# A cross network on one core: x0 transposed from the gathered rows, its rows repeated by DMA, first layer-1 chunk two banks later

## The chip, the core and the metric

One core of a Trainium2 chip. Its engines run their own queues and meet at semaphores: TensorE (PE, with its weight loads PEld), VectorE (DVE), ScalarE (ACT), GpSimd (POOL) and SyncE (SP), which here only issues DMAs. The metric is the time of one launch in microseconds on the device, median of several runs. A single execution was also recorded by the hardware profiler, and all rows below come from it.

## What is computed

A batch of 1024 samples. For each, 39 embedding rows of 16 numbers are gathered from 39 tables (x0: 39 x 16). Three layers of a compressed interaction network follow, then a small dense tower:

```python
for W in [f0, f1, f2]:                       # W: (39*g, 128), g = 39, 128, 128
    z = einsum('bfd,bgd->bfgd', x0, xk).reshape(b, 39 * g, d)
    xk = einsum('bpd,pm->bmd', z, W)         # 128 maps of 16 numbers
    outs.append(xk)
z = sum(concatenate(outs, axis=1), axis=-1)  # (b, 384)
h = relu(concatenate([z, dense_ctx]) @ W_top1 + b_top1)
h = relu(h @ W_top2 + b_top2)
y = h @ W_top3
```

## The kernel before

The kernel works on columns (sample, d). A batch is 128 samples, 2048 columns; there are 8. A batch has 4 groups of 512 columns, and a group has 4 tiles of 128 columns. `step(bt, u, last)` is one tile on each engine: TensorE, VectorE and ScalarE run u = 0 and 1 of batch 0, then a loop of seven batches with u = 2 to 17, then the rest. Within a step ten banks q = 0 to 9 follow each other, and the tables of pairs at the top of the file, (tile in the group, bank) or (u, bank), say behind which bank an extra piece of work is put. So the order is written out by hand, engine by engine.

Layer 2, `cin2`, is the bulk: for a tile, y = x1 times the weights of four fields, in three matmuls of 512 columns per bank (high and low parts, L456, L457, L460; the tenth bank has 384). Banks live in a ring of five (`RING`), so bank n waits until bank n-5 has been used up. Banks 0, 3, 5 and 7 are scaled by ScalarE (`scale`, L664), the others by VectorE in multiply-adds (`mac`, L809), four per bank. GpSimd adds up the 16 terms (`add_up`, L351, L355) into x2; `terms` and x2 have two buffers, so the sum of tile u must be there before ScalarE scales tile u+2. VectorE's second bank waits for ScalarE's first.

Layer 1, `cin1`, is for the next group: seven chunks k of 117 rows, each the product of two factors of x0. `x0_cols` holds x0 by columns with its 39 fields repeated cyclically, 123 rows, so that factor k is rows k to k+117. SP moves the factors: `move_first` (three DMAs, into `x0_first`, which ScalarE copies to PSUM, L643) and `move` (six DMAs into `prods`, L292). VectorE multiplies (`multiply`, L781) at the places `PRODUCTS`, ScalarE splits three of them (L648), GpSimd makes the low parts (L219), and TensorE does the chunks at the places `CIN1`: the first at (1, 6), which waits for all seven products (L424). Three chunks take three short matmuls, the others one fp32 matmul.

Layer 3 goes through `sum_s3` (L470) and, once per batch, `cin3` (L480).

The x0 of the next batch: GpSimd gathers one table after the other into `x0_in` (L328), 39 gathers spread over the sums of 15 tiles, u = 10 to 24. At (9, 3) ScalarE copies the rows three times and a bit into `x0_rows` (`put_aside`, L605 and L607; L704 and L838 in the prologue), which frees `x0_in`. At the four places `TURNS`, TensorE transposes them, four transposes each (`turn`, L404, out 123 rows), and ScalarE stores the columns (`store_cols`, L616; `store_first_cols`, L623, in the prologue). SP's queue in the loop: for each group `move`, with `move_first` of the next, then `move_diag`, eight DMAs; ahead of group 4 it loads the ids of the batch after next.

## Time and profile before

| | us |
|---|---|
| median of 3 runs | 1400.6 (1400.31 to 1401.37) |
| the profiled execution | 1401.89 |
| its span | 1400.1 |
| TensorE busy | 1297.8 |
| GpSimd busy | 1040.9 |
| VectorE busy | 981.8 |
| ScalarE busy | 773.4 |

Some 52 us at the start are the serial gathers of batch 0 and some 60 at the end are the dense tower; between them the program is periodic, with eight batches of four groups. The granted clock of TensorE is 1.00 of its full speed nearly throughout. A busy TensorE is not one at its peak: matmuls overlap, and a row's duration is longer than its distance to the next.

### The profile page before, as it was taken

To read this page: it belongs to the slowest core of one execution; us is meant where nothing else is said; L and a number is where in the kernel's file an instruction comes from. 1 tells how busy PE (TensorE), PEld (TensorE's weight loads), DVE (VectorE), ACT (ScalarE), POOL (GpSimd) and SP (SyncE) were. 2 spreads that over 40 slices of the span, in tenths; PEclk is the share of its full clock that TensorE was granted. 3 is DMA by queue.
4 is the path that set the end of the run, shared out by engine and by line. 5 is a ranking of instruction groups with operands and counts; after the bars stand their busy time and mean duration, and the time that the engine had idled before them with its cause. 6 is when DMAs were issued, how large, how long until landed. Compare 5 with 4: busy or idle time off the path is not lost.

```text
span 1400.1 us, 25243 instructions
## 1 busy us (share of the span) xinstructions
PE 1297.8 (93%) x5629; PEld 982.7 (70%) x5629; DVE 981.8 (70%) x3243; ACT 773.4 (55%) x2449; POOL 1040.9 (74%) x921
## 2 busy tenths in 40 slices
PE   0199999999999999999999999999999999999999
PEld 0167677876787777777777777777778777777754
DVE  2078778586877878587876878688786878688720
ACT  2146666356646665467655566466664576456631
POOL 7668888686887878788886888788786866566530
PEclk9999999999999999999999999999999999999999
DMA  8122121110211121011211112111211101111000
GB/s 218 36 82 55 47 59 53 37 43 24 59 54 51 46 59 53 5 53 46 60 53 51 46 33 58 28 53 46 60 52 52 46 12 55 45 51 45 1 1 0
DMA packets 72379, 67.51 MB, mean 48 GB/s; under 512 B 32140, under 2 KB 44402, under 8 KB 72260
## 3 DMA queue, kind: packets, MB, share of 16 engines
q1 hardware_dynamic: 59556, 62.38, 15.0%
q0 software_dynamic: 9984, 2.58, 1.9%
q10 hardware_dynamic: 2720, 1.48, 0.4%
q14 instruction: 107, 0.88, 0.2%
q8 instruction: 12, 0.20, 0.1%
HBM read 10.15 MB, written 0.00 MB: 7 GB/s over the span
## 4 chain that ended last, share of the span: by engine, by line
PE 65%; DVE 15%; issue 10%; POOL 5%; ACT 2%; DMA 1%; DVEq 1%; SPq 0%; ACTq 0%; POOLq 0%
PE ps L456 13%; PE ps L460 13%; PE ps L457 13%; PE ps L435 13%; DVE terms L809 10%; PE ps L480 5%; DVE prods L781 4%; POOL x_in L328 3%; PE ps L470 3%; PE ps L545 2%; ACT terms L664 2%; PE ps L404 2%; POOL terms L351 2%; PE ps L555 1%; DVEq L808 1%
## 5 line engine op out<-in xcount | busy, mean ns | idle before, releaser
L809 DVE SCALAR_TENSOR_TENSOR terms<-ps,x_scal,terms 128x128 f32<-128x128 f32 x2944 | 814.8, 344 | 294.2 <-PE ps L460 182.6
L664 ACT ACTIVATE terms<-ps,x_scal 128x128 f32<-128x128 f32 x2048 | 586.1, 375 | 388.9 <-PE ps L460 359.8
L351 POOL TENSOR_TENSOR terms<-terms 128x1024 f32<-128x1024 f32 (+2 forms) x384 | 565.6, 1473 | 173.7 <-DVE terms L809 152.9
L456 PE MATMUL ps<-w_high,x_high 128*128 128x512 f32 (+1 forms) x1280 | 581.6, 454 | 3.8 <-ACT terms L664 1.7
L460 PE MATMUL ps<-w_high,x_low 128*128 128x512 f32 (+1 forms) x1280 | 498.7, 390 | 1.1 <-ACT x_rows L607 1.1
L457 PE MATMUL ps<-w_low,x_high 128*128 128x512 f32 (+1 forms) x1280 | 498.3, 389 | 0.0
L328 POOL DMA_INDIRECT x_in<-in_tbl,ids_now x312 | 299.8, 961 | 97.7 <-issue 86.1
L456 PEld LDWEIGHTS ps<-w_high,x_high 128*128 128x128 f32 x1280 | 240.9, 188 | 97.1 <-DVE terms L809 21.7
L457 PEld LDWEIGHTS ps<-w_low,x_high 128*128 128x128 f32 x1280 | 241.6, 189 | 73.5 <-issue 29.8
L460 PEld LDWEIGHTS ps<-w_high,x_low 128*128 128x128 f32 x1280 | 240.9, 188 | 54.5 <-ACT x_rows L607 2.0
L435 PE MATMUL ps<-prods,w 117*128 117x512 f32 x262 | 135.3, 602 | 5.0 <-DVE prods L781 5.0
L781 DVE TENSOR_TENSOR prods<-prods,ps 117x512 f32<-117x512 f32 x192 | 130.4, 679 | 2.3 <-DMA prods<-x_cols 2.3
L219 POOL TENSOR_TENSOR prods_low<-prods,prods_high 117x512 fp32r<-117x512 f32 x93 | 119.0, 1296 | 16.4 <-DMA ids_now<-in_ids 8.6
L470 PE MATMUL ps<-x_diag,x 128*128 128x320 f32 x256 | 89.5, 431 | 0.0
L648 ACT ACTIVATE prods_high<-prods 117x512 fp32r<-117x512 f32 x93 | 60.5, 651 | 42.7 <-DVE prods L781 42.7
L480 PEld LDWEIGHTS ps<-s,w 128*128 128x128 f32 x624 | 73.1, 192 | 2.4 <-issue 0.5
L480 PE MATMUL ps<-s,w 128*128 128x128 f32 x624 | 73.2, 275 | 0.0
L355 POOL TENSOR_TENSOR x<-terms 128x128 f32<-128x128 f32 x128 | 58.9, 460 | 17.8 <-POOL terms L351 14.5
L435 PE MATMUL ps<-prods_high,w_high 117*128 117x512 f32 x93 | 39.8, 428 | 33.2 <-DVE prods L781 30.5
L404 PE MATMUL ps<-eye,x_rows 128*123 128x128 f32 x128 | 29.1, 360 | 39.3 <-ACT x_rows L704 39.3
L435 PEld LDWEIGHTS ps<-prods,w 117*128 117x128 f32 x262 | 50.0, 193 | 22.1 <-issue 7.6
L404 PEld LDWEIGHTS ps<-eye,x_rows 128*123 128x123 f32 x128 | 30.0, 299 | 41.0 <-issue 39.8
(49 smaller groups left out, 525.7 us busy)
## 6 DMA issues: line engine op xcount, KB each, us to landing
prods<-x_cols SPq DMA_DIRECT2D x192, 234.0 KB
x_first<-x_cols SPq DMA_DIRECT2D x96, 78.0 KB
x_in<-in_tbl,ids_now POOLq DMA_INDIRECT x312
x_diag<-x_scal SPq DMA_DIRECT2D x256, 9.8 KB
s<-in_f SPq DMA_DIRECT2D x3, 832.0 KB, 13.3
wt<-in_W_top ACTq DMA_DIRECT2D x1, 768.0 KB, 8.1
wt<-in_W_top ACTq DMA_DIRECT2D x1, 512.0 KB, 9.3
terms<-in_w_pair SPq DMA_DIRECT2D x1, 409.5 KB
```

The source lines that it names most:

```text
L219: eng.tensor_tensor(prods_low[:, i, :], prods[0:KR, SPLIT[i], :], prods_high[:, i, :].bitcast(F32), ALU.subtract).then_inc(low_ready(gf, i ...
L328: pool.indirect_dma_start(out=x0_in[:, f, :], out_offset=None, in_=tables[f], in_offset=bass.IndirectOffsetOnAxis(ap=ids_now[:, f:f + 1], ...
L351: nc.gpsimd.tensor_tensor(t[:, 0:n], t[:, 0:n], t[:, n:2 * n], ALU.add).then_inc(s_tree, 1)
L435: mm = nc.tensor.matmul(ps[:, X1_BANK, :], w, x, start=(k == order[0] and n == 0), stop=(k == order[-1] and n == len(passes) - 1))
L456: nc.tensor.matmul(y, x1_high[:, par, at:at + P], high, start=True, stop=False)
L457: nc.tensor.matmul(y, x1_high[:, par, at:at + P], low, start=False, stop=False)
L460: nc.tensor.matmul(y, x1_low[:, par, at:at + P], high, start=False, stop=True) \
L470: nc.tensor.matmul(ps[:, S3_BANK, 0:TB * FX], x2[:, u % 2, :], x0_diag[:, j % 2, t].rearrange("p b f -> p (b f)"), start=True, stop=True). ...
L480: mm = nc.tensor.matmul(ps[:, MISC_BANK, 0:BATCH], w2[:, f, :], s3[:, f, :], start=(f == 0), stop=(f == F - 1))
L664: op = nc.scalar.activation(terms[:, u % 2, FB * ACT_BANKS.index(q) + i, :], ps[:, (BANKS * u + q) % RING, i * G:(i + 1) * G], ACT.Copy, s ...
L781: nc.vector.tensor_tensor(prods[0:KR, k, :], second, ps[0:KR, bank, :], ALU.mult) \
L809: nc.vector.scalar_tensor_tensor(out=acc, in0=y, scalar=x0, in1=acc, op0=ALU.mult, op1=ALU.add).then_inc(s_mac, 1)
```

## The change

Three edits. The transposes read `x0_in` directly, 39 columns each, and `x0_rows`, `put_aside` and VectorE's copies go. `x0_cols` gets rows 0 to 38 from the store, and SP copies them to rows 39 to 77, 78 to 116 and 117 to 122 by three DMAs (`repeat`) and waits for them; in the prologue first for the 512 columns of group 0, then for the other 1536. Since `x0_in` is now in use until the fourth turn, GpSimd's gathers wait for that (`s_turn`) and are spread over u = 11 to 24. Five of the seven places of `CIN1` move: the first from (1, 6) to (1, 8).

```diff
-CIN1 = ((1, 6), (1, 9), (2, 2), (2, 5), (2, 8), (3, 1), (3, 4))
+CIN1 = ((1, 8), (2, 1), (2, 4), (2, 6), (2, 8), (3, 1), (3, 4))
...
-ROWS_AT = (9, 3)
+GATHERED, SUMMED = 8, 10
...
+            def repeat(cols, n):
+
+                for i in range(1, SPT + 1):
+                    rows = min(F, CYCLIC - i * F)
+                    sp.dma_start(x0_cols[i * F:i * F + rows, cols], x0_cols[0:rows, cols]).then_inc(s_cyc, 16)
+                sp.wait_ge(s_cyc, n * (16 * SPT))
...
                 if j == 0:
                     sp.wait_ge(s_cols, 4)
+                    repeat(slice(GCOLS, BATCH * D), 2)
                 if j % GROUPS < GROUPS - 1:
                     move_first(j + 1)
...
             sp.wait_ge(s_cols, 1)
+            repeat(slice(0, GCOLS), 1)
             move(0, 0)
...
                 load_ids(bt + 2)
+                sp.wait_ge(s_cols, bt * 4 + 8)
+                repeat(slice(0, BATCH * D), bt + 3)
                 move(bt * GROUPS + GROUPS, GROUPS)
...
             pool.wait_ge(s_ids, 2 * 16)
-            pool.wait_ge(s_rows, 3)
-            wanted, ahead = ROWS_AT[0], 12
+            pool.wait_ge(s_turn, 4)
+            ahead = 12
...
             with pool.Fori(0, NBATCH - 2) as bt:
                 pool.wait_ge(s_ids, (bt + 3) * 16)
-                pool.wait_ge(s_rows, bt * 2 + 5)
-                add_up(bt, wanted)
-                for n in range(STEPS - 1):
-                    for f in share(0, n, STEPS - 1):
-                        gather(f)
-                    add_up(bt, wanted + 1 + n)
+                pool.wait_ge(s_turn, bt * 4 + 8)
+                add_up(bt, SUMMED)
+                for n in range(1, STEPS):
+                    if n <= GATHERED + STEPS - SUMMED:
+                        for f in share(0, n - 1, GATHERED + STEPS - SUMMED):
+                            gather(f)
+                    add_up(bt, SUMMED + n)
...
                 if r == 0:
-                    pe.wait_ge(s_rows, bt * 2 + 5)
+                    pe.wait_ge(s_gather, bt * (16 * F) + 2 * (16 * F))
                     pe.wait_ge(s_scal, bt * GROUPS + GROUPS)
...
-                rows = x0_rows[:, :].rearrange("p (f d) -> p f d", d=D)
                 for i in range(4):
-                    mm = nc.tensor.transpose(ps[0:CYCLIC, bank, i * P:(i + 1) * P],
-                                             rows[:, :, 4 * r + i], eye[:, :])
+                    mm = nc.tensor.transpose(ps[0:F, bank, i * P:(i + 1) * P],
+                                             x0_in[:, :, 4 * r + i], eye[:, :])
...
-            def put_aside(bt):
...
-                    if not last and (u, q) == ROWS_AT:
-                        put_aside(bt + 1)
```

TensorE, in the loop, around the first chunk of layer 1. L456, L457 and L460 are one bank of `cin2`, ISA and REGISTER_ALU rows set up waits. Before, from the last matmul of (1, 6) on:

```order
L460 MATMUL ps<-w1_high,x1_low 128x512
L424 ISA
L427 ISA
L435 MATMUL ps<-prods_high,w0_high 128x512
L435 MATMUL ps<-prods_high,w0_low 128x512
L435 MATMUL ps<-prods_low,w0_high 128x512
L447 REGISTER_ALU
L456 MATMUL ps<-w1_high,x1_high 128x512
L457 MATMUL ps<-w1_low,x1_high 128x512
```

After, from the last matmul of (1, 7) on; the lines are 13 further down in the file:

```order
L473 MATMUL ps<-w1_high,x1_low 128x512
L458 REGISTER_ALU
L469 MATMUL ps<-w1_high,x1_high 128x512
L470 MATMUL ps<-w1_low,x1_high 128x512
L473 MATMUL ps<-w1_high,x1_low 128x512
L437 ISA
L440 ISA
L448 MATMUL ps<-prods_high,w0_high 128x512
L448 MATMUL ps<-prods_high,w0_low 128x512
L448 MATMUL ps<-prods_low,w0_high 128x512
L460 REGISTER_ALU
L469 MATMUL ps<-w1_high,x1_high 128x384
```

Two banks, (1, 7) and (1, 8), now stand ahead of the chunk, and only (1, 9) follows it in the step.

SP, in the loop, between the moves of group 3 and those of group 4. Before:

```order
L262 ISA [waits rows_gathered]
L262 DMA ids_now<-in_ids 128x39
L270 DMA x0_first<-x0_cols 39x512 [waits x1_summed]
L270 DMA x0_first<-x0_cols 39x512 x2
L292 DMA prods<-x0_cols 117x512 x6
```

After:

```order
L261 DMA ids_now<-in_ids 128x39
L319 REGISTER_ALU
L268 DMA x0_cols<-x0_cols 39x2048 [waits x0_cols_stored]
L268 DMA x0_cols<-x0_cols 39x2048
L268 DMA x0_cols<-x0_cols 6x2048
L269 ISA
L276 DMA x0_first<-x0_cols 39x512 [waits x1_summed,x0_cols_repeated]
L276 DMA x0_first<-x0_cols 39x512 x2
L298 DMA prods<-x0_cols 117x512 x6
```

Three DMAs came in between, and the first factors wait for two things instead of one.

GpSimd, in the loop, between the sums of u = 11 and u = 12. Before:

```order
L355 TENSOR_TENSOR x2<-terms 128x128 [waits s3_summed]
L328 DMA x0_in<-in_tbl_5,ids_now 128x16
L328 DMA x0_in<-in_tbl_6,ids_now 128x16
L218 ISA
L219 TENSOR_TENSOR prods_low<-prods,prods_high 117x512 [waits product_highs_ready]
```

After:

```order
L368 TENSOR_TENSOR x2<-terms 128x128 [waits s3_summed]
L341 DMA x0_in<-in_tbl_2,ids_now 128x16
L341 DMA x0_in<-in_tbl_3,ids_now 128x16
L341 DMA x0_in<-in_tbl_4,ids_now 128x16
L217 ISA
L218 TENSOR_TENSOR prods_low<-prods,prods_high 117x512 [waits product_highs_ready]
```

The gathers run three tables behind those of before here, with three between these sums instead of two.

## Rows read from the trace of the kernel before

**Rows 1.** The page: busy time of each engine, share of the span, instructions.
```profile
PE 1297.8 (93%) x5629; PEld 982.7 (70%) x5629; DVE 981.8 (70%) x3243; ACT 773.4 (55%) x2449; POOL 1040.9 (74%) x921
```

**Rows 2.** TensorE's waits: engine and line, released by; us in total, times, longest.
```profile
PE ps L435 <- DVE prods L781: 35.5, 30, 5.0
```

**Rows 3.** Timeline of TensorE, one group: start, us, line, shapes [idle before <-releaser].
```profile
931.66 0.40 PE L457 MATMUL ps<-w_low,x_high 128*128 128x512 f32 x1
931.90 0.39 PE L460 MATMUL ps<-w_high,x_low 128*128 128x512 f32 x1
933.32 0.50 PE L435 MATMUL ps<-prods_high,w_high 117*128 117x512 f32 x1 [1.04 <-DVE prods L781]
```

**Rows 4.** Timeline of VectorE, the same stretch.
```profile
931.47 1.12 DVE L809 SCALAR_TENSOR_TENSOR terms<-ps,x_scal,terms 128x128 f32<-128x128 f32 x4
932.51 0.68 DVE L781 TENSOR_TENSOR prods<-prods,ps 117x512 f32<-117x512 f32 x1
```

**Rows 5.** The chain that ended last, the same stretch: start, us, what.
```profile
933.32 0.95 PE ps L435 x3
```

**Rows 6.** The chain again: chunk 0 of groups 1 to 3, in batch 0.
```profile
92.75 0.97 PE ps L435 x3
...
129.63 0.95 PE ps L435 x3
...
168.99 0.97 PE ps L435 x3
```

**Rows 7.** Timelines of GpSimd and ScalarE, the last group of a batch.
```profile
1031.07 0.46 POOL L355 TENSOR_TENSOR x<-terms 128x128 f32<-128x128 f32 x1 [0.16 <-POOL terms L351]
...
1033.19 1.14 ACT L664 ACTIVATE terms<-ps,x_scal 128x128 f32<-128x128 f32 x4 [0.78 <-PE ps L460]
```

**Rows 8.** Timeline of GpSimd: gathers of batch 1 and batch 4.
```profile
319.05 0.95 POOL L328 DMA_INDIRECT x_in<-in_tbl,ids_now  x1 [4.69 <-issue]
...
788.85 0.96 POOL L328 DMA_INDIRECT x_in<-in_tbl,ids_now  x1 [2.96 <-issue]
790.12 0.96 POOL L328 DMA_INDIRECT x_in<-in_tbl,ids_now  x1 [0.31 <-issue]
```

**Rows 9.** The chain: matmuls of layer 3, and one turn of x0.
```profile
897.13 2.90 PE ps L480 x26
...
971.84 0.74 PE ps L404 x4
```

**Rows 10.** Timeline of the prologue, all engines; the DMA's row is from the chain.
```profile
56.29 1.24 ACT L704 ACTIVATE x_rows<-x_in 128x1248 f32<-128x1248 f32 x1 [31.84 <-DMA x_in<-in_tbl,ids_now]
57.68 3.75 PE L404 MATMUL ps<-eye,x_rows 128*123 128x128 f32 x16 [39.34 <-ACT x_rows L704]
62.51 2.53 SPq L270 DMA_DIRECT2D x_first<-x_cols  x3
77.86 4.96 SPq L292 DMA_DIRECT2D prods<-x_cols  x6
83.08 0.68 DVE L781 TENSOR_TENSOR prods<-prods,ps 117x512 f32<-117x512 f32 x1
...
64.30 2.41 DMA x_first<-x_cols
```

**Rows 11.** Timelines of SP's queue and ScalarE where a batch's columns are replaced.
```profile
991.75 2.51 SPq L270 DMA_DIRECT2D x_first<-x_cols  x3
...
985.33 1.04 ACT L616 ACTIVATE x_cols<-ps 123x512 f32<-123x512 f32 x1 [0.30 <-PE ps L404]
...
997.34 0.62 ACT L643 ACTIVATE ps<-x_first 117x512 f32<-117x512 f32 x1
```

**Rows 12.** Windows of 1 us: busy us (x) by engine, PEclk, DMA share, GB/s.
```profile
993.00:994.00 1.00, 1.00 (x6) 0.78 (x5) 0.89 (x3) 0.94 (x4) 0.79 (x2) 1.00 0.30 80
999.00:1000.00 1.00, 1.00 (x7) 0.79 (x5) 1.00 (x4) 0.65 (x2) 0.92 (x2) 1.00 0.79 242
```

More of the change, by code:

```diff
@@ L313, in _ @@
             for gf in range((NBATCH - 2) * GROUPS + 1, NGROUP):
+                if gf % GROUPS == 0:
+                    sp.wait_ge(s_cols, 4 * NBATCH)
+                    repeat(slice(0, BATCH * D), NBATCH + 1)
                 move(gf, gf % GROUPS or GROUPS)
@@ L364, in _ @@
             pool.wait_ge(s_ids, 2 * 16)
-            pool.wait_ge(s_rows, 3)
-            wanted, ahead = ROWS_AT[0], 12
+            pool.wait_ge(s_turn, 4)
+            ahead = 12
             for f in range(ahead):
                 gather(f)
-            for u in range(wanted):
-                if u < wanted - 1:
-                    for f in share(ahead, u, wanted - 1):
+            for u in range(SUMMED):
+                if u < GATHERED:
+                    for f in share(ahead, u, GATHERED):
                         gather(f)
```

31 lines of the change are left out of this document (7 added, 24 removed).

## The prediction

> **What bounds the kernel now.** I read the page's list of engines first: TensorE is busy 93% of the span, GpSimd 74% [rows 1]. So the question is where TensorE still stands, and the waits say it: 35.5 us in 30 waits at L435 (the layer-1 matmuls of `cin1`), put down to VectorE's products of L781 [rows 2]. I call a unit of 512 columns a group: there are 32, and `cin1` runs inside the loop for 31 of them. The timeline of TensorE in one group shows the place: the last matmul of bank (1, 6) starts at 931.90 and the first of chunk 0 at 933.32, 1.04 us idle [rows 3]. VectorE's timeline beside it shows why: product 6, the last of seven, runs at 932.51, right behind the four multiply-adds of bank (1, 2), which start at 931.47, and VectorE has no gap between them [rows 4]. Chunk 0 asks for all seven products, so the chain of waits runs through them once per group [rows 5].
>
> A period of a plain group is 36.9 us (92.75 to 129.63 in the chain) [rows 6]. The second engine to watch is GpSimd. It sums the 16 terms of each tile and issues 39 gathers per batch between the sums. Its sum of tile u must be ready before ScalarE's first scaling of tile u+2. In the last group of a batch, the sum ends at 1031.07 + 0.46 = 1031.53 and ScalarE starts at 1033.19: a slack of 1.66 us only [rows 7].
>
> **Part 1: the first chunk two banks later.** TensorE will run banks (1, 7) and (1, 8) ahead of chunk 0. Counting from the row of (1, 6), TensorE is ready for (1, 7) at 931.90 + 0.23 = 932.1. But the y banks are a ring of five: (1, 7) overwrites (1, 2), which VectorE frees at 931.47 + 1.12 = 932.59 [rows 4]. So the wait doesn't go, it shrinks: about 0.5 us at the bank ring instead of 1.2. Then: (1, 7) from 932.6 with 0.7 for its three matmuls and 0.2 for the start after a wait (the chain has 0.95 for the three matmuls of chunk 0 behind its wait [rows 5], where three follow each other at 0.23 to 0.24, as 931.66 to 931.90 [rows 3]), to 933.5; (1, 8) to 934.2; chunk 0 to 934.9; (1, 9), of 384 columns, 0.53, to 935.43. (1, 9) needs bank (1, 4), four multiply-adds (1.1 us) behind product 6, which ends by 933.2: free near 934.3, no wait [rows 4]. In the kernel before the same work is done at 933.32 + 0.95 for chunk 0, 1.40 for the two banks and 0.53 for (1, 9): 936.20 [rows 5]. The gain is 0.78 us per group. Behind it (2, 1) wants (1, 6), free at 935.3, and gets there at 936.1; the other chunks lie between banks as before.
>
> Where that doesn't count: in batch 0 GpSimd already sets the pace. From 129.63 to 168.99 the group takes 39.4 instead of 36.9 [rows 6], since there 27 gathers are squeezed into eight tiles. I take the gain of the first two groups as lost. 29 x 0.78 = 22.6 us.
>
> **Part 2: the gathers in 14 tiles instead of 15.** By the order, the tile ahead of u = 12 gets 3 gathers instead of 2, and the gathers start one tile later. One gather more is 1.27 us of GpSimd (0.96 and 0.31 of issue, at 790.12) [rows 8]. The slack of 1.66 at the batch's last group falls by 1.27, and by the 0.78 that TensorE comes sooner: -0.4. ScalarE's (0, 0) comes 0.4 late, VectorE starts behind it and is the saturated one: 0.4 x 6 batches = 2.4 us lost. In two places GpSimd stood still for 4.69 and 2.96 us ahead of a gather, which the profile puts to issue [rows 8]; I don't know the cause and assume that they come again. With 2.0 us less slack behind them up to 4 us more are lost; I take 3. The new wait of GpSimd, on the fourth transposition, stands ahead of the sum of u = 10, whose terms end later anyway: nothing. The wait for the ids moves with it, off the tile u = 9.
>
> **Part 3: transposes of 39 columns.** Four turns per batch of four transposes each, in seven batches, lie on TensorE's path, at 0.74 us each [rows 9]. TensorE streams the same 128 columns; only the weights shrink. Bounds: nothing saved, or down to the rate of L480's matmuls of 128 columns (2.90/26 = 0.11 each, 0.45 a turn) [rows 9]. The nearest row is the second: the same 128 columns of stream behind a load of 128 columns at 0.11, so the 0.185 of a transpose must hang on something else than the stream, and the load of rows that lie 64 bytes apart is what is left. I take 0.25 us saved a turn, nearly all: 28 x 0.25 = 7 us (range 0 to 8). The 16 transposes of the prologue take 0.23 each [rows 10]; I leave them as they are. The Trainium skill (TensorE: Matmul & The Clock Gate, "LDWEIGHTS (loading the stationary operand)") says that a weight load takes time by its columns, about 1 ns for 1.2 columns; for 39 columns it would be hidden behind the stream and the turn would fall to the lower bound. No row of this trace shows 39 columns.
>
> ScalarE's `put_aside`, once a batch, lies beside TensorE's work in an engine that is busy 55% [rows 1]: nothing.
>
> **Part 4: the prologue.** It is serial: gather landed, copy of the rows, 16 transposes, store, moves. The copy of 1.24 us and its hand-over go: transposes could start at 56.3 instead of 57.68, -1.4 [rows 10]. Behind the store come three repeats and a wait for all of them. Three like DMAs, L270, were issued from 62.51, and the last of them, issued at 64.30, took 2.41 more: 4.2 us [rows 10]. That is +2.8. Then SP has a second repeat of three in its queue, ahead of `move_first(1)`, the eight DMAs of x0_diag and `move(1)`: 2.3 us of issue and 2.4 of landing. SP works through this queue without a pause, so `move(1)` starts at 77.86 + 2.8 + 4.7 = 85.4, and its first part lands near 87.8 at the soonest. VectorE wants it at 83.08 + 2.8 = 85.9 [rows 10]. +1.9 to 2.6, and all of it goes on, since GpSimd's pace in batch 0 starts with that tile. Together +5 us.
>
> **Part 5: the repeat in each batch.** SP issues it when the fourth store is done (985.33 + 1.04 = 986.4) and waits for it ahead of `move_first`, whose release was at 991.75 [rows 11]. Three issues of 0.76 and a landing of 2.4 end at 990.4; 688 KB (39 + 39 + 6 rows of 8 KB) at the 242 GB/s that the moves of 117 rows reach [rows 12] take 2.8 us, within that or 0.5 more. Free by about 1 us; behind it the three first factors would land at 993.3 + 2.4 = 995.7, and ScalarE takes them at 997.34: 1.6 us more [rows 11]. Nothing.
>
> **Sum.** 22.6 + 7 - 2.4 - 3 - 5 = 19 us. The profiled execution of before took 1401.9 us (span 1400.1); minus 19 is 1383. The median of the three runs is 1.3 us below the profiled one: 1382.
>
> **Rivals.**
> A. GpSimd becomes the bound (15%). The slack of 1.66 us is what TensorE's old pace left it [rows 7], and part 2 turns it negative. If the lateness comes up in each gathering group instead of staying at 0.4 per batch, the gathering groups keep the old period and only those without it gain: four of the last batch and one of each of the others, some 12 x 0.78 = 9.4, with the turns 7, less 5 and 3: 8 less, 1392. For it: batch 0, where just that is seen [rows 6]. Against it: batch 0 has 3.4 gathers a tile, the others 2.8, and the group with layer 3 lets GpSimd catch up.
> B. The repeat is slow (12%). The only second in which DMAs of 39 rows ran alone shows 80 GB/s against 242 for those of 117 rows [rows 12]. At half of the high rate, 121 GB/s, 688 KB take 5.7 us, the repeat lands near 993.8, 2.1 us after the release, 0.5 more than the slack of 1.6: 3.5 us in seven batches and 2 more in the prologue: 1388. The Trainium skill (SBUF — State Buffer, "Door 1: The DMA port swizzle") says that partitions 0 to 63 reach 8 of the 16 ports, so a copy out of rows 0 to 38 would run at half the rate; by that rule B would be the case.
> C. Slower than before (6%). The same mechanism at 80 GB/s: 688 KB take 8.6 us, the repeat lands near 997, 5.2 us after the release; 3.6 us beyond the slack, x 7 = 25, and 4 in the prologue: 1383 + 29 = 1411. It decides from about 2.7 us beyond the slack per batch, a rate of some 90 GB/s. Against it: while those 80 GB/s ran, the engines were busy 0.30 of the time only [rows 12]; they waited for issues.
> D. The whole wait goes (7%): the ring lets (1, 7) in, 29 x 1.04 = 30 us, and GpSimd keeps up: 1401.9 - 30 - 7 + 5 = 1370, by the median 1369.
> E. The shift does nothing, since the next bank stands just as long (4%): turns and prologue are left, 1401.9 - 7 + 5 - 1.3 = 1399.
>
> **How the numbers follow.** The forecast, the small wait at the bank ring, has 56%; A 15, B 12, C 6, D 7, E 4. The range reaches from near D, 1373, to just over A, 1393; C and E are outside, and D. A measurement here can tell some 0.2%, 2.8 us, from no change: faster (under 1397.8) is the forecast with A, B, D: 0.90; same 0.04; slower 0.06.
>
> **What would show it.** In the profile after: the wait at L448 (the new line of L435's matmul) all but gone and one at the first matmul of a bank, on VectorE's multiply-adds, of some 0.5 us per group; plain groups of 36.1 us; turns near 0.5; the second DMA-fed product of group 1, at 83.08 before, 5 us later; the last repeat landing before the release of `move_first`. Wrong it would be if waits on GpSimd's L368 or L218 grow to tens of us (A), or if `move_first` comes late behind the repeat (B, C).

## The result, and the profile after

The changed kernel takes 1393.8 us (median of 5 runs, 1392.9 to 1394.0) against 1401.4 us for the kernel before in the same session: a ratio of 0.9945, 95% interval 0.9931 to 0.9960. It is faster, by 7.5 us or half a per cent, clear of the noise. Forecast were 1382 us and a gain of 19; 1393.8 lies above the range's end of 1393. The profiled execution has a span of 1391.3 us against 1400.1.

TensorE's busy time and GpSimd's have hardly changed, against [rows 1]:

```profile
PE 1294.6 (93%) x5629; PEld 971.1 (70%) x5629; DVE 978.5 (70%) x3241; ACT 760.4 (55%) x2434; POOL 1038.3 (75%) x921
```

The waits of TensorE (engine and line, released by; us in total, times, longest) are to be read beside [rows 2]. In the changed kernel L448 is the matmul of layer 1, L469, L470 and L473 are the three passes of a y bank in layer 2, L619 is ScalarE's store of a turn, L805 VectorE's multiply-add:

```profile
PE ps L469 <- DVE terms L805: 18.6, 34, 5.1
PE ps L448 <- DVE prods L777: 8.6, 1, 8.6
PE ps L473 <- ACT x_cols L619: 5.6, 6, 1.1
```

The 35.5 us at layer 1 have become 8.6, all of it one wait in the prologue; 34 waits stand at the bank ring instead, one of 5.1 us in batch 0 and most of the others near 0.37; and a third line is new: six waits for a store of ScalarE, one per batch in batches 1 to 6. TensorE's timeline in the group of [rows 3] shows the first of these changes (start, us, line, shapes, idle before and its releaser):

```profile
929.92 0.50 PE L469 MATMUL ps<-w_high,x_high 128*128 128x512 f32 x1 [0.37 <-DVE terms L805]
...
931.19 0.40 PE L473 MATMUL ps<-w_high,x_low 128*128 128x512 f32 x1
931.42 0.40 PE L448 MATMUL ps<-prods_high,w_high 117*128 117x512 f32 x1
```

Bank (1, 7) waits 0.37 us for VectorE's multiply-adds of (1, 2), and chunk 0 (931.42) follows (1, 8)'s last matmul with no gap. The turn in the chain of waits, beside [rows 9], went from 0.74 to 0.44:

```profile
975.11 0.44 PE ps L417 x4
```

So the two parts that were meant to gain have gained. To see where it was lost, I use ScalarE's copy of the first factor, which runs once at the start of each group, as a ruler. In the changed kernel's timeline of ScalarE:

```profile
994.42 0.60 ACT L646 ACTIVATE ps<-x_first 117x512 f32<-117x512 f32 x1 [1.21 <-DMA x_first<-x_cols]
...
1029.93 0.62 ACT L646 ACTIVATE ps<-x_first 117x512 f32<-117x512 f32 x1
```

The copies before these two start at 917.93 and 954.05. A plain group lasts 954.05 - 917.93 = 36.12 us, where it was 957.51 - 920.65 = 36.86 before. The group in which x0 of the next batch is turned lasts 994.42 - 954.05 = 40.37 us (39.83 before), and the one behind it 35.51 (36.86 before). Taken together the last two are only 0.81 us shorter, where two chunk shifts (0.74 each) and four turns (0.30 each) should have brought 2.68.

Two places in that stretch are late. The first is where GpSimd's pace shows. Timelines of GpSimd, ScalarE and TensorE around the start of tile 10 (L341 is a gather, L368 a tile's sum x2, L667 ScalarE's scaling):

```profile
961.22 0.96 POOL L341 DMA_INDIRECT x_in<-in_tbl,ids_now  x1 [0.21 <-issue]
...
963.73 0.95 POOL L341 DMA_INDIRECT x_in<-in_tbl,ids_now  x1 [0.30 <-issue]
964.70 2.53 POOL L218 TENSOR_TENSOR prods_low<-prods,prods_high 117x512 fp32r<-117x512 f32 x2
967.18 4.59 POOL L364 TENSOR_TENSOR terms<-terms 128x1024 f32<-128x1024 f32 x3
971.93 0.46 POOL L368 TENSOR_TENSOR x<-terms 128x128 f32<-128x128 f32 x1 [0.16 <-POOL terms L364]
...
972.50 1.14 ACT L667 ACTIVATE terms<-ps,x_scal 128x128 f32<-128x128 f32 x4 [3.38 <-POOL x L368]
973.52 1.03 ACT L619 ACTIVATE x_cols<-ps 39x512 f32<-39x512 f32 x1
...
974.60 0.50 PE L473 MATMUL ps<-w_high,x_low 128*128 128x512 f32 x1 [0.86 <-ACT x_cols L619]
```

Three gathers, two low halves, three tree steps and the sum take GpSimd 11.2 us for a tile that TensorE does in 9.0. ScalarE stands 3.38 us at its first scaling of tile 10, and in its queue behind that scaling is the store of the second turn. TensorE, which may not turn again into the same bank before it, waits 0.86 us at (10, 4).

That one tile doesn't make all of the lateness. GpSimd's timeline earlier in the batch, at the terms of tile 2 and the sum of tile 3:

```profile
908.36 4.56 POOL L364 TENSOR_TENSOR terms<-terms 128x1024 f32<-128x1024 f32 x3 [4.07 <-DVE terms L805]
...
922.58 0.46 POOL L368 TENSOR_TENSOR x<-terms 128x128 f32<-128x128 f32 x1 [0.16 <-POOL terms L364]
```

In the group with layer 3 GpSimd still waits for VectorE, 4.07 us at tile 2 and 0.63 at tile 3, so there it has caught up. From the end of tile 3's sum (923.04) to that of tile 8's (972.39) it never waits longer than the 0.3 us between two gathers. It takes 49.35 us for these five tiles, 9.87 each, and a plain group goes by at 9.03 a tile: 4.2 us are lost over five tiles.

The second is the repeat of the columns by DMA, with the move behind it (chain of waits, start, us, what):

```profile
982.12 0.87 SPq L268
983.05 0.81 SPq L268
983.91 6.50 DMA x_cols<-x_cols
990.42 0.79 SPq L276
...
992.04 2.36 DMA x_first<-x_cols
```

From the first issue to the landing it takes 8.3 us, and the first factor comes 1.21 us late for ScalarE. Windows of 1 us in it (busy us and count by engine, PEclk, DMA share, GB/s):

```profile
984.00:985.00 1.00, 1.00 (x5) 0.58 (x4) 0.57 (x3) 0.31 (x2) 1.00 (x1) 1.00 0.84 213
987.00:988.00 1.00, 1.00 (x6) 0.80 (x5) 1.00 (x4) 0.74 (x2) 0.92 (x2) 1.00 0.21 33
```

The bytes flow at 213 GB/s in the best microsecond, close to the 242 of [rows 12], and then a few late packets trail along at 33. Over the whole 8.3 us, 688 KB are 83 GB/s.

The last place is the prologue (timelines of SyncE's queue and VectorE; L268 repeats, L276 moves a first factor, L313 fills x0_diag, L298 moves the second factors):

```profile
71.88 3.17 SPq L268 DMA_DIRECT2D x_cols<-x_cols  x3
79.59 2.35 SPq L276 DMA_DIRECT2D x_first<-x_cols  x3
82.06 5.24 SPq L313 DMA_DIRECT2D x_diag<-x_scal  x8
87.53 4.96 SPq L298 DMA_DIRECT2D prods<-x_cols  x6
...
90.95 0.69 DVE L777 TENSOR_TENSOR prods<-prods,ps 117x512 f32<-117x512 f32 x1 [5.01 <-DMA prods<-x_cols]
```

VectorE's first product with a moved factor runs at 90.95 instead of 83.08 [rows 10]: 7.9 us later.

### The profile page after: what moved, and what is told of

It reads as the page before. It is cut to its first block, busy times and chain, and to the rows that moved or that the text cites. A ratio compares the mean times of both kernels' runs of the same rounds, so it can differ in the third digit from the quotient of the medians.

```text
span 1391.3 us, 25265 instructions
## 1 busy us (share of the span) xinstructions
PE 1294.6 (93%) x5629; PEld 971.1 (70%) x5629; DVE 978.5 (70%) x3241; ACT 760.4 (55%) x2434; POOL 1038.3 (75%) x921
## 3 DMA queue, kind: packets, MB, share of 16 engines
q0 software_dynamic: 9984, 2.58, 2.2%
## 4 chain that ended last, share of the span: by engine, by line
PE 50%; POOL 14%; DVE 11%; issue 10%; DMA 6%; ACT 5%; SPq 3%; DVEq 1%; POOLq 0%; ACTq 0%
PE ps L469 10%; PE ps L473 10%; PE ps L470 10%; PE ps L448 9%; DVE terms L805 9%; POOL terms L364 6%; POOL x_in L341 5%; PE ps L493 5%; DMA x_cols<-x_cols 4%; ACT terms L667 3%; DVE prods L777 3%; PE ps L558 2%; PE ps L483 2%; POOL prods_low L218 2%; DMA x_first<-x_cols 1%
## 5 line engine op out<-in xcount | busy, mean ns | idle before, releaser
L805 DVE SCALAR_TENSOR_TENSOR terms<-ps,x_scal,terms 128x128 f32<-128x128 f32 x2944 | 811.6, 346 | 276.0 <-PE ps L473 149.3
L667 ACT ACTIVATE terms<-ps,x_scal 128x128 f32<-128x128 f32 x2048 | 585.8, 375 | 388.6 <-PE ps L473 342.1
L469 PE MATMUL ps<-w_high,x_high 128*128 128x512 f32 (+1 forms) x1280 | 592.5, 463 | 24.3 <-DVE terms L805 18.6
L473 PE MATMUL ps<-w_high,x_low 128*128 128x512 f32 (+1 forms) x1280 | 499.7, 390 | 6.1 <-ACT x_cols L619 5.6
L470 PE MATMUL ps<-w_low,x_high 128*128 128x512 f32 (+1 forms) x1280 | 497.8, 389 | 0.0
L341 POOL DMA_INDIRECT x_in<-in_tbl,ids_now x312 | 298.9, 958 | 100.5 <-issue 84.6
L469 PEld LDWEIGHTS ps<-w_high,x_high 128*128 128x128 f32 x1280 | 241.4, 189 | 136.5 <-DVE terms L805 50.5
L470 PEld LDWEIGHTS ps<-w_low,x_high 128*128 128x128 f32 x1280 | 242.4, 189 | 71.0 <-issue 29.8
L473 PEld LDWEIGHTS ps<-w_high,x_low 128*128 128x128 f32 x1280 | 241.2, 188 | 60.2 <-ACT x_cols L619 8.2
L448 PE MATMUL ps<-prods,w 117*128 117x512 f32 x262 | 135.3, 601 | 8.6 <-DVE prods L777 8.6
L368 POOL TENSOR_TENSOR x<-terms 128x128 f32<-128x128 f32 x128 | 58.8, 459 | 17.8 <-POOL terms L364 15.3
L448 PEld LDWEIGHTS ps<-prods,w 117*128 117x128 f32 x262 | 49.3, 193 | 22.7 <-issue 11.7
L679 ACT ACTIVATE s<-ps 128x320 f32<-128x320 f32 x128 | 58.4, 456 | 0.6 <-PE ps L483 0.6
L483 PEld LDWEIGHTS ps<-x_diag,x 128*128 128x128 f32 x256 | 48.3, 189 | 11.5 <-issue 0.5
L777 DVE TENSOR_TENSOR prods<-x_cols,ps 117x512 f32<-117x512 f32 x32 | 21.8, 680 | 48.9 <-ACT ps L646 48.9
```

The source lines that it names most:

```text
L341: pool.indirect_dma_start(out=x0_in[:, f, :], out_offset=None, in_=tables[f], in_offset=bass.IndirectOffsetOnAxis(ap=ids_now[:, f:f + 1], ...
L448: mm = nc.tensor.matmul(ps[:, X1_BANK, :], w, x, start=(k == order[0] and n == 0), stop=(k == order[-1] and n == len(passes) - 1))
L469: nc.tensor.matmul(y, x1_high[:, par, at:at + P], high, start=True, stop=False)
L470: nc.tensor.matmul(y, x1_high[:, par, at:at + P], low, start=False, stop=False)
L473: nc.tensor.matmul(y, x1_low[:, par, at:at + P], high, start=False, stop=True) \
L483: nc.tensor.matmul(ps[:, S3_BANK, 0:TB * FX], x2[:, u % 2, :], x0_diag[:, j % 2, t].rearrange("p b f -> p (b f)"), start=True, stop=True). ...
```

## Theory and rivals

My theory after this comparison: the chunk shift and the turns are worth what I see in plain groups, in some 30 groups 30 x 0.74 = 22 us, and 28 x 0.30 = 8 us. Three things take 22 of these 30 back: (a) GpSimd, which over the 14 tiles with gathers needs more time than TensorE now gives it; (b) the repeat, too late for the next batch's first factor; (c) the second repeat in the prologue, three times as large as my estimate allowed for. The rival is that (a) is only an accident of the order of ScalarE's queue, and another, that the gain never was 22 but is lost in ring waits or on VectorE.

Each experiment was timed beside the kernel before, whose median was between 1400.9 and 1401.4 us each time; a difference between two runs below is one of medians, and half a microsecond of it can be this. All times are medians. Line numbers in their rows are those of each kernel itself, a few lines off from the changed one's.

## Experiments

**The chunk shift alone.** The kernel before with one line changed:

```
-CIN1 = ((1, 6), (1, 9), (2, 2), (2, 5), (2, 8), (3, 1), (3, 4))
+CIN1 = ((1, 8), (2, 1), (2, 4), (2, 6), (2, 8), (3, 1), (3, 4))
```

> The kernel before with one line changed: the new places of the seven layer-1 chunks (CIN1). Turns, aside copy and x0_rows are as before. Theory: the chunk shift is worth what the changed kernel's plain groups show, 36.86 - 36.12 = 0.74 us a group, and nothing else here takes it back, since the rows set aside let the first move start as before: 30 x 0.74 = 22 us, so 1379 us, up to 1382 if ScalarE's wait for GpSimd now reaches TensorE's turns here too (1.1 us in some batches). The longer turn group of the changed kernel (40.35 against 39.83 us) should be gone: about 39.1 us. Rival (GpSimd sets the pace of a batch once TensorE is faster): at most half of it arrives, 1390 us, and TensorE waits for x2 or for the terms in more places.

1389.7 us against 1401.2 (ratio 0.9918, 0.9904 to 0.9931): 11.5 us of the 22, which is the rival's number, not mine. It is also better than the whole change. In the turn group ScalarE now waits for the last gather before it can put the rows aside, and TensorE waits for that (timelines of ScalarE and TensorE):

```profile
961.24 1.77 ACT L605 ACTIVATE x_rows<-x_in 128x1872 f32<-128x1872 f32 x1 [0.77 <-DMA x_in<-in_tbl,ids_now]
...
963.31 0.50 PE L460 MATMUL ps<-w_high,x_low 128*128 128x512 f32 x1 [0.25 <-ACT x_rows L607]
```

It is 0.25 us here; in the two batches with a standstill of GpSimd (below) it is 2.29 and 2.05. The turn group stays at 39.69 us against 39.83, so the shift's 0.74 is lost there. I had expected this only of the changed kernel. The same shortage of GpSimd shows itself with the old transposes too, at another place.

**The change without the chunk shift.** The changed kernel with the old line for `CIN1`.

> The changed kernel with the old places of the chunks (CIN1), so that only the new turns and the repeat by DMA remain of the change. Theory: the chunk shift gave 30 x 0.74 = 22 us, of which the turn group's wait for ScalarE's store (0.86 us and its refill, 1.1 us in each of 7 batches) goes away again, since GpSimd has more time: 1394 + 22 - (0 to 8) = 1408 to 1416 us, slower than the kernel before (1401) by what the prologue (8.4 us) and the late move (0.75 us x 7) cost beyond the shorter turns (0.30 us x 28 = 8.4 us). Rival (the chunk shift's gain is partly eaten by GpSimd, so undoing it costs less): 1402 us, level with the kernel before.

1406.6 us (ratio 1.0038, 1.0024 to 1.0052): slower than the kernel before, as the theory had it, but by 5.4 instead of 7 to 15 us. The rest of the change costs 5.4 us by itself, and undoing the shift costs 12.8, again little more than half of 22. The wait of [rows 2] is back, with 35.8 us in 27 times.

**The repeat in two parts.** The first part covers group 0's columns only; the rest goes behind the move of group 0:

```
-                repeat(slice(0, BATCH * D), bt + 3)
-                move(bt * GROUPS + GROUPS, GROUPS)
-                move_diag(bt * GROUPS + GROUPS, GROUPS)
+                repeat(slice(0, GCOLS), bt * 2 + 3)
+                move(bt * GROUPS + GROUPS, GROUPS, bt * 2 + 4)
...
+                if rest is not None:
+                    move_diag(gf, j)
+                    repeat(slice(GCOLS, BATCH * D), rest)
                 if j % GROUPS < GROUPS - 1:
                     move_first(j + 1)
```

> The changed kernel with the repeat of each batch in two parts, as its prologue has it: first only the 512 columns of the next batch's group 0, then the move of that group, and the other 1536 columns behind the move. Theory: the repeat's 8.3 us before the move (982.12 to 990.41) make VectorE's first product late (0.59 us for the first factor, 0.75 us a batch in all); with a quarter of the bytes it should take 4 us, the first factor lands about 4 us earlier, and TensorE's group gains 0.75 us in each of 7 batches: 1394 - 5 = 1389 us. Rival (the first factor is late only beside something else that is as late, GpSimd's low halves or the turn's wait): no change, 1394 us. The two waits of the changed kernel, ScalarE for x_first (1.21 us) and VectorE for that copy (0.59 us), must be gone under both.

1390.6 us (0.9924, 0.9910 to 0.9937), 3.2 us better than the changed kernel. The first factor is no longer late (timelines of SyncE's queue and ScalarE):

```profile
980.84 2.47 SPq L268 DMA_DIRECT2D x_cols<-x_cols  x3
986.28 2.37 SPq L276 DMA_DIRECT2D x_first<-x_cols  x3
...
991.80 0.62 ACT L650 ACTIVATE ps<-x_first 117x512 f32<-117x512 f32 x1
```

It takes 5.4 us for a quarter of the bytes (I expected 4), ScalarE's wait is gone, and the two groups together take 39.00 + 36.53 = 75.53 us instead of 75.88: 0.35 us a batch, where I had read 0.75 off VectorE's idle time. A late first factor costs TensorE less than VectorE's wait shows.

**The second turn two banks sooner.**

```
-TURNS = ((9, 7), (10, 0), (10, 4), (10, 8))
+TURNS = ((9, 7), (9, 9), (10, 4), (10, 8))
```

> The changed kernel with the second turn at (9,9) instead of (10,0), so that ScalarE's store of it no longer stands behind scale(10,0), which waits 3.38 us for GpSimd's x2. Theory: TensorE's wait at (10,4) for that store (0.86 us with about 0.25 us of refill, 1.1 us a batch) goes, and nothing takes its place, since VectorE's ring wait is met by then: 7 x 1.1 = 8, so 1386 us. Rival (GpSimd is the bound there, and the wait only moves): TensorE waits the same microsecond at the next chunk or at the sum of the last tile (x2), 1394 us. Second rival: ScalarE is too slow to have stored the first turn by (9,9), and the wait moves two banks forward with a quarter of its size: 1388 us.

1387.7 us (0.9904, 0.9889 to 0.9919): 6.1 us gained by moving four matmuls. The store is now ahead of the scaling in ScalarE's queue, and the wait at (10, 4) is gone from TensorE's list. ScalarE still waits for GpSimd there:

```profile
967.39 2.28 ACT L667 ACTIVATE terms<-ps,x_scal 128x128 f32<-128x128 f32 x8 [1.29 <-POOL x L368]
```

The two groups take 39.54 + 35.50 = 75.04 us, 0.84 less than 75.88. So the place in ScalarE's queue is what lets GpSimd's lateness through to TensorE, in the changed kernel.

**The repeat in thirds, in the prologue too.** `move` of group 0 is followed by the repeat of group 1's columns alone; the last 1024 columns are repeated in the move of group 1:

```
                 if j == 0:
                     sp.wait_ge(s_cols, 4)
-                    repeat(slice(GCOLS, BATCH * D), 2)
+                    repeat(slice(GCOLS, 2 * GCOLS), 2)
+                if j == 1:
+                    repeat(slice(2 * GCOLS, BATCH * D), rest)
```

> The changed kernel with the repeat cut in three everywhere: group 0's columns first, group 1's behind the move of group 0, the last 1024 columns in the move of group 1. In the batches this is the split of the run before it (1390.6 us); new is the prologue, where the second repeat now takes 512 columns instead of 1536 before the first factor of group 1 is moved. Theory: the repeat of 1536 columns took 7.7 us (71.88 to 79.57) and pushed the move of group 1 and VectorE's first product behind it (90.95 against 83.08 us); with a third of the bytes about 4 us of the lateness go: 1390.6 - 4 = 1387 us. Rival (the start is late by the eight diagonal moves and GpSimd's gathers, and the product's wait only moves to these): no better than the split alone, 1390.6 us.

1387.4 us (0.9902, 0.9887 to 0.9917), 3.2 us better than with two parts. The prologue (SyncE's queue and VectorE):

```profile
71.90 2.57 SPq L268 DMA_DIRECT2D x_cols<-x_cols  x3
76.61 2.35 SPq L276 DMA_DIRECT2D x_first<-x_cols  x3
...
84.56 4.96 SPq L298 DMA_DIRECT2D prods<-x_cols  x6
...
87.85 0.69 DVE L784 TENSOR_TENSOR prods<-prods,ps 117x512 f32<-117x512 f32 x1 [2.67 <-DMA prods<-x_cols]
```

The repeat of 512 columns takes 71.90 to 76.61 = 4.7 us instead of 7.7, exactly what the prediction had put down for the larger one, and the product comes 3.1 us sooner. SyncE then works without a pause: eight issues for x0_diag (5.2 us) stand ahead of the moves that VectorE waits for.

**Rows of 2 KB instead of 8.** Every repeat in the batches as six transfers, each of every other 512 columns.

```
+                    for b in range(2):
+                        to, of = (x0_cols[r, cols].rearrange("k (a b x) -> k a b x", a=2, b=2)[:, :, b, :]
+                                  for r in (slice(i * F, i * F + rows), slice(0, rows)))
+                        sp.dma_start(to, of).then_inc(s_cyc, 16)
```

> The changed kernel with the repeat of each batch as six transfers of rows of 2 KB (every other 512 columns) instead of three of 8 KB; the same 688 KB, between the same partitions. Theory (84 packets of 8 KB are five or six in a row on each of 16 DMA engines, and the longest of them, 2.1 us, hold the end): with 336 packets the engines share the bytes evenly, and from the first issue to the last landing it takes 6 us instead of 8.3, with three more issues of some 0.6 us in it; time 1392 us. Rival (39 partitions can take no more than 90 to 170 GB/s, whatever the packets): 8.3 us or more, the transfers 592 ns x 1/4 = 150 ns a packet on average against 77 undisturbed, and 1394 us or slower.

1391.8 us (0.9937, 0.9922 to 0.9952), an interval that overlaps the changed kernel's. The chain:

```profile
980.99 0.90 SPq L274
...
985.36 3.64 DMA x_cols<-x_cols
989.01 0.82 SPq L282
```

From first issue to landing 8.0 us instead of 8.3. What comes behind the last issue has shrunk from 6.5 to 3.6 us, so long packets did make a tail of some 3 us; but the three more issues cost 2.6 us. The packets took 142 ns on average, twice the shortest (81 ns), where 84 packets of the same size in the split repeat took 114. So the theory is right on the tail, the rival is nearer on the sum (6 and 8.3 were expected), and the time doesn't tell them apart. Fewer bytes ahead of the move is the cure, not smaller rows.

**Fewer gathers.** Batches 2 to 7 gather 26 of the 39 tables; the rows left out are those of an earlier batch, and the semaphore counts are adapted:

```
                         for f in share(0, n - 1, GATHERED + STEPS - SUMMED):
-                            gather(f)
+                            if f % 3:
+                                gather(f)
```

> The changed kernel in which batches 2 to 7 gather only 26 of the 39 tables (every third is left out, so the rows of an earlier batch stand there); GpSimd saves 13 x 1.25 = 16 us a batch. Theory (GpSimd falls behind over the 14 tiles in which it gathers: 2.8 gathers x 1.25 + 0.97 for the low halves + 5.2 for the tree and x2 = 9.7 us a tile against TensorE's 9.03, so that ScalarE's scale at the start of tile 10 waits 3.4 us and holds the store of a turn, and the two hiccups of 3 to 4 us find no slack): TensorE's wait at (10,4) goes (1.1 us in each of 6 batches) and the hiccups' 2 to 4 us with it, 1394 - 7 - 5 = 1382 us, batches of 155.5 us with none of 160. Rival (only the one store's place in ScalarE's order matters): as with the early turn, 1387.7 us.

1378.4 us (0.9838, 0.9825 to 0.9851): 15.4 us less than the changed kernel, more than the 12 expected, with the slow repeat and the late prologue still in it. This is the largest effect of any single edit. ScalarE's waits for GpSimd go from 41.1 us in 16 waits to

```profile
ACT terms L668 <- POOL x L368: 7.3, 3, 3.2
```

and every batch from 1 to 6 lasts 155.7 us, where the changed kernel had 156.8 and two of 160.8 and 159.8 us (by the same ruler). The two groups take 39.24 + 35.46 = 74.70 us. Hence GpSimd costs the changed kernel 75.88 - 74.70 = 1.18 us in each of six batches, and its two standstills 4.0 and 3.0 us on top: 14 us. The edit also takes away a quarter of the bytes that gathers move in all (1.93 MB for 2.58 MB, of 73 MB). That this is not what counts is shown by the next run, in which all gathers are made.

**The gathers over 15 tiles.** The first share goes ahead of the sum of tile 10, as before the change (a step on a semaphore of its own stands between the wait and the first gather):

```
                 pool.wait_ge(s_turn, bt * 4 + 8)
-                add_up(bt, SUMMED)
-                for n in range(1, STEPS):
+                for n in range(STEPS):
                     if n <= GATHERED + STEPS - SUMMED:
-                        for f in share(0, n - 1, GATHERED + STEPS - SUMMED):
+                        for f in share(0, n, GATHERED + STEPS - SUMMED + 1):
                             gather(f)
                     add_up(bt, SUMMED + n)
```

> The changed kernel with the gathers of a batch spread over 15 tiles instead of 14: the first share goes ahead of the sum of tile 10 (where GpSimd waits 4.7 us for VectorE's terms), as in the kernel before. Theory (GpSimd's lag at tile 8 builds up over the gathering tiles): the lag shrinks by 1 to 3 us, ScalarE's wait for x2 before scale(10,0) falls from 3.4 to about 1, TensorE's wait at (10,4) goes in most batches and part of the hiccups: 1394 - 7 = 1387 us. Rival (GpSimd catches up anyway in its idle stretches between the tiles, and only the last share of three gathers counts): 1394 us.

1388.6 us (0.9911, 0.9895 to 0.9926), 5.2 us gained. ScalarE's waits for GpSimd fall to

```profile
ACT terms L668 <- POOL x L369: 16.6, 7, 3.9
```

and TensorE's wait at (10, 4) is gone in the batches without a standstill. GpSimd is late at tile 10 even so. The wait there is no longer in this list, because the profile puts it to TensorE:

```profile
968.68 1.15 ACT L668 ACTIVATE terms<-ps,x_scal 128x128 f32<-128x128 f32 x4 [2.10 <-PE ps L474]
```

But it ends 0.11 us behind the end of the sum (968.57), just as the one of 3.38 us did (972.50 and 972.39). So it is GpSimd's still, shorter by 1.3 us. That is one gather: tiles 4 to 8 have 13 instead of 14. Moving the gathers to 14 tiles cost 5.2 us; the prediction set 2.4 aside for it and 3 more for the standstills. The last share of three gathers is the same in both kernels, so it isn't what makes the lag.

**The two controls: is it GpSimd that halves the chunk shift?** The kernel before, and the kernel with the chunk shift alone, each with 26 of 39 gathers in batches 2 to 7.

> The kernel before, in which batches 2 to 7 gather only 26 of the 39 tables (every third left out). Theory (before the change GpSimd keeps up everywhere but for its two hiccups): its batches are 159.13 us, and those with a hiccup 163.35 and 160.22; without 13 gathers GpSimd has 16 us of slack and both become about 159.1: 1401 - 4.2 - 1.1 = 1396 us. Rival (GpSimd holds TensorE back by a little in every tile already): every batch shorter by 1 us or more, 1390 us or less.

> The chunk shift alone (the kernel before with the new CIN1) and only 26 of the 39 gathers in batches 2 to 7. Read against the run before it, with the same gathers and the old CIN1: what the chunk shift gives where GpSimd is not behind. Theory (the shift is worth its 0.74 us in each of 30 groups and loses half only to GpSimd's lag): 1396 - 22 = 1374 us, batches of about 156.2 us with no wait of TensorE for the rows put aside. Rival (half of the shift's gain is lost to something else, ring waits or VectorE): 1396 - 11 = 1385 us.

1395.8 us (0.9967, 0.9955 to 0.9980) and 1376.8 us (0.9829, 0.9815 to 0.9843). The kernel before gains 5.2 us, which is its two standstills (its plain batches stay at 159.1 us): GpSimd did not hold it back otherwise. With GpSimd relieved the chunk shift is worth 1395.8 - 1376.8 = 19.0 us instead of 11.5. That is near the 22 of the theory and far from the rival's 11. Batches go from 159.1 to 156.4, 2.7 of the 2.96 us. Batch 0, whose gathers I left in full, gains nothing: the copy of the first factor for batch 1 starts at 195.54 us against 195.31. Of the 7.5 us between 11.5 and 19.0, five lie in the two batches with a standstill (162.51 and 160.60 us with all gathers and 156.42 and 156.39 with 26, where the old places have 163.35 and 160.22 against 159.23 and 159.11), and two in the four others. So most of what the shift lost, it lost because no slack was left behind the standstills. TensorE's waits in the two kernels, old places and new:

```profile
PE ps L436 <- DVE prods L782: 37.9, 32, 5.2
```

```profile
PE ps L457 <- DVE terms L810: 12.8, 33, 0.7
```

**All three repairs.** Repeat in thirds, second turn at (9, 9), gathers over 15 tiles.

> The three repairs on the changed kernel together: the repeat in thirds (alone 1387.4 us), the second turn at (9,9) (alone 1387.7) and the gathers over 15 tiles (alone 1388.6). Theory: the last two cure the same wait, so only the larger of them counts and what the split gives in the batches is there in any case: 1387.4 - 6.5 = 1381 us, batches near the 155.7 us of the run with fewer gathers. Rival (they add in full): 1387.4 - 6.1 - 5.2 = 1376 us. Second rival (the gathers ahead of tile 10 delay its sum once TensorE is faster): 1385 us.

1377.6 us (0.9835, 0.9822 to 0.9849), 16.3 us less than the changed kernel. The theory said 1381 and the rival, full addition, 1376; the sum of the three single gains is 6.4 + 6.1 + 5.2 = 17.7. I was wrong to think that the turn and the gathers cure the same thing: the turn group is down to 38.15 us, the lowest of the runs so far, and ScalarE's wait at tile 10 is down to 0.16 us. My reading is that the earlier turn removes the way by which lateness reaches TensorE, and the longer spread removes lateness. The two groups take 74.29 us, 0.41 less than with fewer gathers, near the 0.35 that the repeat alone gave.

**The diagonal moves on ScalarE's queue.** As the last one, with the prologue's eight moves for x0_diag issued by ScalarE behind its first copy of a first factor:

```
                 store_first(0, 0, FIRST_BANK)
+                act.wait_ge(s_ones, 1)
+                act.wait_ge(s_scal, 1)
+                for b in range(TB):
+                    rows = slice(b * D, (b + 1) * D)
+                    act.dma_start(x0_diag[rows, 0, :, b, 0:F], x0_scal[rows, 0, :, :]).then_inc(s_diag[0], 16)
                 store_x1(0, 0)
```

> The run before it, with the first group's eight diagonal moves (SyncE's 79.09 to 84.32 in the run with the repeat in thirds) issued on ScalarE's queue, which is idle from 69.3 to 78.1 us. Theory (the order of SyncE's issues sets VectorE's first product of group 1, at 87.9 us): the moves of group 1 are issued 5.2 us sooner and the start gains up to 5 us: 1381 - 5 = 1376 us, or somewhat less, since ScalarE's copy of the first factor and GpSimd come next. Rival (GpSimd with its 39 gathers in batch 0 sets the end of that batch anyway): within 1 us of the run before it.

1375.0 us (0.9815, 0.9801 to 0.9829): 2.5 us, half of what was expected. ScalarE's and SyncE's queues and VectorE:

```profile
68.96 7.18 ACTq L717 DMA_DIRECT2D x_diag<-x_scal  x8
...
80.33 4.83 SPq L299 DMA_DIRECT2D prods<-x_cols  x6
...
85.66 0.68 DVE L785 TENSOR_TENSOR prods<-prods,ps 117x512 f32<-117x512 f32 x1
```

The moves are issued at 80.33, and the product runs at 85.66 with no wait ahead of it, where it was at 88.50 in the run before: 2.8 us. Behind it VectorE works on with hardly a gap until 99 us, so the other half of the 5.2 us finds no use there. This kernel is the best of all: 26.0 us under the kernel before and 18.8 under the changed one.

## Why the prediction was wrong, point by point

Three steps of the prediction failed. Part 2 looked for GpSimd's lateness at one place, where none came, and set 5.4 us aside for what costs 8.8. Part 4 priced the prologue's second repeat like the first, 4.7 us, and it took 7.7. Part 5 put the repeat in each batch at nothing, and it costs some 2.4 us in all. The gain on TensorE itself was forecast rightly.

Medians of the runs that changed these groups, and the two groups that hold the turns and the repeat (start of ScalarE's copy to the next but one):

| kernel | us | turn group + next, us |
|---|---|---|
| before | 1401.0 | 39.83 + 36.86 = 76.69 |
| changed | 1393.8 | 40.37 + 35.51 = 75.88 |
| chunk shift alone | 1389.7 | 39.69 + 36.17 = 75.86 |
| repeat in two parts | 1390.6 | 39.00 + 36.53 = 75.53 |
| second turn sooner | 1387.7 | 39.54 + 35.50 = 75.04 |
| gathers over 15 tiles | 1388.6 | 39.51 + 35.48 = 74.99 |
| 26 gathers | 1378.4 | 39.24 + 35.46 = 74.70 |
| three repairs | 1377.6 | 38.15 + 36.14 = 74.29 |

**Part 1, the chunk shift: mechanism and size right, what it sets off missed.** Forecast were a wait of about 0.5 us at the ring and plain groups 0.78 us shorter; measured are 0.37 and 0.74. But 29 x 0.78 took for granted that the others follow. It yields 11.5 us in the kernel before, and 12.8 in the changed kernel, because GpSimd doesn't follow. Where it is relieved, it yields 19.0, and most of the rest is batch 0, where three groups gain nothing and not two.

**Part 2, GpSimd: the wrong place, and too little.** The prediction looked at the slack in one place, the batch's last group [rows 7], found -0.4 us and multiplied by six. At that place nothing was lost:

```profile
1028.07 0.46 POOL L368 TENSOR_TENSOR x<-terms 128x128 f32<-128x128 f32 x1 [0.16 <-POOL terms L364]
...
1028.91 1.14 ACT L667 ACTIVATE terms<-ps,x_scal 128x128 f32<-128x128 f32 x4 [0.77 <-PE ps L473]
```

The sum ends at 1028.53, and ScalarE starts 0.38 us later, behind a wait for TensorE. The lateness came at the start of tile 10, where ScalarE stood 3.38 us. The prediction should have compared rates over the stretch where the load is highest. On average over the 14 tiles GpSimd has 39/14 gathers of 1.25 us, 0.97 us of low halves and 5.2 for tree and sum, 9.7 us in all, against TensorE's 9.03; in tiles 4 to 8 it measured 9.87. It costs 1.18 us in each of six batches instead of 0.4, and through a chain (x2, scaling, store of a turn, TensorE) that was not in the prediction. With the standstills it is 14 us of the changed kernel's time, of which 5.2 were in the kernel before already: 8.8 are new, where 2.4 + 3 were set aside.

Rival A, at 15%, had the right engine and the right kind of fault, a rate. Its 1392 us are near the result, but in part by luck: it let all gathering groups keep their old period, and the plain ones among them, as that from 917.93 to 954.05, gained their full 0.74 us. Its sign, ScalarE's waits for x2, went from 25.4 us in 12 waits to 41.1 in 16. The argument against it, that the group with layer 3 lets GpSimd catch up, was true (the 4.07 us at tile 2), but five tiles later it was behind again.

**The standstills.** They did come again. The batch with the first is as much shorter than before as the others, 163.35 to 160.83 us; the one with the second gained only 0.4 and so lost some 1.9. Forecast were 3 us for both.

**Part 3, the turns: right.** 0.74 to 0.44 instead of 0.49; about 8 us instead of 7. The Trainium skill (TensorE: Matmul & The Clock Gate, "LDWEIGHTS (loading the stationary operand)") says that a weight load's time goes by its columns, and the prediction gave 0.45 as the turn by that rule; the trace agrees with 0.44. The loads themselves took 302 ns with 123 columns and 144 with 39 (medians of 128 each). But those of L480, with 128 columns that lie side by side, took 192 ns. So the number of columns alone doesn't order these times. The columns of a turn lie 64 bytes apart, before and after, and no run here separates that from their number.

**Part 4, the prologue: one term mis-sized.** The copy's 1.4 us went (transposes at 56.15). The first repeat took 3.8 us for 4.2 forecast. The second was priced at 4.7 like the first, though it has three times the bytes: it took 7.7. The run with thirds gave back just these 3 us. At the start of batch 1 the changed kernel is 238.77 - 233.00 = 5.8 us behind, where the steps together allowed 5 - 2 x 0.78 - 1.0 = 2.4. The 3.4 us between are mainly that term of 3.0 and the gain that the third group of batch 0 didn't make.

**Part 5, the repeat in a batch: the tail missed.** "Free by about 1 us" rested on 242 GB/s and a landing of 2.4 us. The rate was nearly there for a microsecond (213 GB/s), but the last issue took 6.5 us to land, because the last packets trail. From first issue to landing it was 8.3 us, where the forecast had 4.0, rival B 7.4 and rival C, the one slower than before, 10.6. So B came true as well, for a reason of its own: its 0.5 us a batch stand against 0.35 to 0.41 measured, and its 2 us in the prologue against 3. The Trainium skill (SBUF — State Buffer, "Door 1: The DMA port swizzle") gives 8 of the 16 ports, which is all that rows 0 to 38 reach, an upper rate of some 218 GB/s. The trace agrees as far as it goes: its best microsecond shows 213. Half of 242, by which the prediction got B's time, was not the limit. That B's 7.4 us are near the measured 8.3 is luck, since B has no tail. (In rival C, 1383 + 29 is 1412, and 1411 only with the 1.3 for the median taken off.)

**The sum.** By the ruler the profiled execution can be added up in full; it gained 8.8 us (spans), where the terms of the forecast make 19.2.

| stretch | forecast, us | measured, us |
|---|---|---|
| to the second copy of batch 1 | -2.4 | -5.8 |
| six turn groups with the next one | 10.0 | 5.1 |
| the fourteen other groups | 10.9 | 8.7 |
| the rest | 0.8 | 0.7 |

A turn group with its next one was to gain two shifts and four turns, 2.56 us, six times, and the 5.4 us set aside for GpSimd are taken off in this row. The first row misses 3.4 us by the prologue and batch 0, the third 2.2, nearly all in the one group with the second standstill (38.31 us instead of 36.13). The second misses 4.9. By my estimate from the runs 1.2 of them are GpSimd's, beyond the 5.4 (with 26 gathers these six pairs gain 16.7 us instead of 5.1, and in the kernel before 4.9 by the same edit), some 2.4 the repeat's (0.35 to 0.41 six times), and 1.8 the 0.3 us a batch named below; the better turns give some back. What isn't settled: 0.3 us per batch between the best kernel's 155.3 us and the 155.0 that 159.1 less four shifts and four turns would give, and the cause of the standstills.

## What to carry to other kernels

When one engine is made faster, compare for every other engine its work per period with the new period, over the stretch in which its load is highest, and not its slack at one point or its share of the whole span (GpSimd was busy 75%). Then look at what is queued behind the instruction at which the slow engine is waited for: an unrelated store in that queue is how its lateness reaches the bound. And a transfer ahead of which others wait should carry only the bytes that the next step needs.

## What the runs showed of the hardware

GpSimd's standstills go by the count of gathers, not by time or place, in all fourteen traces. In the kernel before they stand ahead of the 114th and the 227th gather (319.05 and 788.85 us [rows 8]); in the changed kernel ahead of the same two, at 324.54 and 787.85; and with 26 gathers a batch ahead of the same two again, but at 403.52 and 1079.61:

```profile
324.54 0.95 POOL L341 DMA_INDIRECT x_in<-in_tbl,ids_now  x1 [4.26 <-issue]
...
787.85 0.94 POOL L341 DMA_INDIRECT x_in<-in_tbl,ids_now  x1 [3.26 <-issue]
```

```profile
403.52 0.95 POOL L341 DMA_INDIRECT x_in<-in_tbl,ids_now  x1 [3.26 <-issue]
...
1079.61 0.95 POOL L341 DMA_INDIRECT x_in<-in_tbl,ids_now  x1 [2.95 <-issue]
```

That is after 113 gathers and after 226, for 3.0 to 5.4 us. With 26 gathers they cost nothing: all batches are as long. I didn't find out what happens there.

A transfer of 39 + 39 + 6 rows of 8 KB inside SBUF had packets of 592 ns on average, from 307 to 2139; it landed 6.5 us after its last issue in all seven batches. Eight small transfers that SyncE's queue issued in 5.2 us took ScalarE's 7.2 the one time that it issued them (68.96, in the last run).
